# One step order for all eight batches in a fused four-stage kernel, with five subtractions moved from GpSimd to VectorE

## The reference

```python
x = x + L0(x)   # x @ W_base.T + b_base + 2 * sum_e w[b,e] * (x @ As[e].T) @ Bs[e].T
x = x + L1(x)   # x @ (sum_g y[b,g] * weight[g] * mask).T + bias
x = x + L2(x)   # two of eight experts by softmax and top-2, weighted, and one shared expert:
                #   (gelu(x @ gate) * (x @ up)) @ down,  128 -> 512 -> 128
x = x + L3(x)   # one expert by argmax: (silu(x @ W_up.T + b_up) * (x @ W_gate.T + b_gate)) @ W_down.T + b_down
```

## Time and profile before

| | us |
|---|---|
| median of three runs | 82.08 |
| profiled execution, own time | 81.98 |
| its span | 80.3 |
| TensorE busy | 75.9 |
| VectorE busy | 53.9 |
| GpSimd busy | 50.3 |
| ScalarE busy | 49.2 |

### The profile page before, as it was taken

One profiled execution on the slowest core, in us unless ns is written; L12 is line 12 of the kernel. 1 busy time (PEld: TensorE's weight loads), 2 busy tenths in 40 slices (PEclk: granted clock), 3 DMA queues, 4 the chain that ended last, 5 costly groups with the idle time before them and its releaser, 6 DMA issues.

```text
span 80.3 us, 1590 instructions
## 1 busy us (share of the span) xinstructions
PE 75.9 (95%) x480; PEld 68.0 (85%) x480; DVE 53.9 (67%) x118; ACT 49.2 (61%) x99; POOL 50.3 (63%) x48
## 2 busy tenths in 40 slices
PE   6999999999999999999994999999999999997990
PEld 6979998888888998988882989989989989996990
DVE  1489679969565638177796939499399498436371
ACT  6420796879855896737999069456496550539160
POOL 3021366298999999999999999985639910000000
DMA  1998288999999995599988998989999679882102
GB/s 17 320 380 343 45 309 328 392 426 429 425 392 411 383 395 203 126 377 347 382 226 231 361 354 295 245 316 301 382 340 270 201 179 232 289 198 63 52 21 65
DMA packets 9367, 22.17 MB, mean 276 GB/s; under 512 B 1040, under 2 KB 5776, under 8 KB 9360
## 3 DMA queue, kind: packets, MB, share of 16 engines
q1 hardware_dynamic: 9072, 21.30, 77.9%
q10 hardware_dynamic: 288, 0.79, 2.5%
HBM read 17.88 MB, written 0.52 MB: 229 GB/s over the span
## 4 chain that ended last, share of the span: by engine, by line
PE 80%; DMA 8%; SPq 5%; DVE 2%; issue 1%; ACT 1%
PE bank L964 16%; DMA x_t<-p 8%; PE bank L950 5%; PE bank L947 5%; PE bank L948 5%; PE bank L979 5%; SPq L259 5%; PE bank L900 5%; PE bank L908 5%; PE bank L916 5%; PE bank L937 4%; PE bank L994 4%; PE bank L831 4%; PE bank L839 3%; PE bank L869 2%; PE bank L923 2%
## 5 line engine op out<-in xcount | busy, mean ns | idle before, releaser
L362 POOL TENSOR_TENSOR pair_low<-pair_w,wide_h 128x512 fp32r<-128x512 f32 x18 | 22.7, 1291 | 3.2 <-ACT wide_h L457 3.2
L419 ACT ACTIVATE gelu<-bank 128x512 f32<-128x512 f32 x24 | 14.1, 594 | 10.2 <-PE bank L950 7.1
L694 DVE SCALAR_TENSOR_TENSOR hid<-gelu,wsel,bank 128x512 f32<-128x512 f32 x16 | 11.8, 735 | 6.2 <-PE bank L950 2.0
L947 PE MATMUL bank<-wide_h,x_h 128*128 128x512 f32 x28 | 11.5, 409 | 0.0
L367 POOL TENSOR_TENSOR hid_l<-hid,hid_h 128x512 fp32r<-128x512 f32 x8 | 10.2, 1289 | 1.8 <-ACT hid_h L470 1.8
L948 PE MATMUL bank<-wide_h,x_l 128*128 128x512 f32 x28 | 10.9, 390 | 0.0
L708 DVE STREAM_TRANSPOSE p<-hid 128x512 f32<-128x512 f32 x14 | 10.0, 712 | 1.1 <-DMA x_t<-p 0.7
L457 ACT ACTIVATE wide_h<-pair_w 128x512 fp32r<-128x512 f32 x18 | 10.4, 622 | 0.4 <-DMA pair_w<-in_skill 0.2
L429 ACT ACTIVATE half<-bank,half_bias 128x128 f32<-128x128 f32 x12 | 3.7, 364 | 8.7 <-PE bank L979 4.4
L692 DVE TENSOR_TENSOR hid<-gelu,bank 128x512 f32<-128x512 f32 x8 | 5.5, 685 | 3.6 <-POOL hid_l L367 2.7
L964 PE MATMUL bank<-x_t,pair_w 128*128 128x128 f32 x40 | 5.5, 280 | 1.6 <-DMA x_t<-p 1.6
(11 more groups left out here) (120 smaller groups left out, 160.1 us busy)
## 6 DMA issues: line engine op xcount, KB each, us to landing
pair_w<-in_skill SPq DMA_DIRECT2D x11, 768.0 KB, 6.9
w<-in_layer SPq DMA_DIRECT2D x6, 384.0 KB, 8.9
x_t<-p SPq DMA_DIRECT2D x16, 128.0 KB, 3.3
b_mix<-p SPq DMA_DIRECT2D x12, 128.0 KB, 4.3
shared_sb<-in_skill SPq DMA_DIRECT2D x1, 768.0 KB, 11.8
home_x<-in_skill SPq DMA_DIRECT2D x1, 768.0 KB, 12.6
home_h<-in_skill SPq DMA_DIRECT2D x1, 768.0 KB, 4.4
home_l<-in_skill SPq DMA_DIRECT2D x1, 768.0 KB, 6.6
```

Of the source, the lines that this page charges most:

```text
L362: pool.tensor_tensor(low_of(b, k)[:, m, :], w[:, m, :], wide_h[:, ring_at(b, k) % RING, m, :].bitcast(fp32), ALU.subtract).then_inc(wide_l ...
L419: act.activation(gelu[:, n, :], ps[:, :], ACT.Gelu_apprx_tanh).then_inc(gelu_ready, 1)
L694: dve.scalar_tensor_tensor(hid[:, n, :], gelu[:, n, :], wsel[:, bass.DynSlice(weight, 1)], u_ps[n][:, :], ALU.mult, ALU.mult).then_inc(hid ...
L947: pe.matmul(ps[:, :], x2_h[:, S * b:S * (b + 1)], wide_h[:, n % RING, m, :], start=True, stop=False)
```

## The change

Batch 0 joins `TURNED`: its experts are done wide, transposed and swapped as the others' are. With that the ring's places, GpSimd's and ScalarE's lists and the loads begin with batch 0. All batches now have one order of steps. Of the eight low parts of the shared hidden values, three stay on GpSimd and five go to VectorE (`hidden_rest`), in the places shown. The last batch's swap goes to a buffer of its own, two tiles of a weight home that batch 2 used, so it waits for nothing but its transposes. `layer3(6)` and `down3(5)` change places with the last batch's `down`.

```diff
-TURNED = range(1, B)
+TURNED = range(B)
+POOL_LOW = 3
...
+        hid_last = pair_w[:, 4, 0:2, :].rearrange("c m (a k s) -> c (m a) k s", k=TOP_K, s=S)
...
         def up3_ps(b, c):
+            if b == B - 2:
+                return (bank[4], bank[7])[c]
             return (bank[3], bank[2])[c] if is_last(b) else bank[7]
...
+        def hid_t_of(b):
+            return hid_last if is_last(b) else hid_t[b % 2]
...
                     sp.wait_ge(turned_ready, TOP_K * (b - TURNED[0] + 1))
-                    if b - 2 in TURNED:
+                    if is_last(b):
+                        sp.wait_ge(down_done, down_at(2, 0))
+                    elif b - 2 in TURNED:
                         sp.wait_ge(down_done, down_at(b - 2, 1))
...
-                for b, k in ((1, 0), (0, 1), (1, 1)):
-                    pick(b, k)
-                    load(b, k)
-                for b, k in ((2, 0), (2, 1), (3, 0)):
+                for b, k in ((0, 1), (1, 0), (1, 1), (2, 0), (2, 1), (3, 0)):
                     pick(b, k)
                     load(b, k)
...
+                swap(0)
                 sp.wait_ge(down_done, NSH)
                 load(4, 1)
+                swap(1)
                 load(5, 0)
                 load(5, 1)
-                swap(1)
-                sp.wait_ge(down_done, down_at(0, 0))
-                load(6, 0)
                 swap(2)
                 sp.wait_ge(down_done, down_at(0, 1))
+                load(6, 0)
                 load(6, 1)
...
-                for k in range(3):
-                    hidden_low_part(k)
-                wide_low_part(1, 0, 0)
-                hidden_low_part(3)
-                hidden_low_part(4)
-                wide_low_part(1, 0, 1)
-                hidden_low_part(5)
-                hidden_low_part(6)
-                wide_low_part(1, 1, 0)
-                hidden_low_part(7)
-                wide_low_part(1, 1, 1)
+                wide_low_part(0, 0, 0)
+                hidden_low_part(0)
+                hidden_low_part(1)
+                wide_low_part(0, 0, 1)
+                hidden_low_part(2)
+                wide_low_part(0, 1, 0)
+                wide_low_part(0, 1, 1)
...
+                rounds = {1: (0, 0, 1), 3: (0, 1, 0), 4: (0, 1, 1), 5: (1, 0, 0), 6: (1, 0, 1), 7: (1, 1, 0)}
+                round_part(0, 0, 0)
                 gelu_step(0, 0, shg_ps[0])
                 for k in range(1, NSH):
                     gelu_step(k, k % 2, shg_ps[k % 3])
                     round_hidden(k - 1)
-                    if k in (3, 4):
-                        round_part(1, 0, k - 3)
-                    if k == NSH - 1:
-                        round_part(1, 1, 0)
+                    if k in rounds:
+                        round_part(*rounds[k])
+                expert_gelu(0, 0)
                 round_hidden(NSH - 1)
-                expert_gelu(0, 0)
                 round_part(1, 1, 1)
                 expert_gelu(0, 1)
...
-                    if 2 <= k < NSH + 2:
-                        dve.wait_ge(hid_low, k - 1)
-                    elif NSH + 2 <= k < NSH + 4:
-                        dve.wait_ge(down_done, down_at(0, n))
+                    if 2 <= k < POOL_LOW + 2:
+                        dve.wait_ge(hid_low_pool, k - 1)
+                    elif POOL_LOW + 2 <= k < NSH + 2:
+                        dve.wait_ge(hid_low_dve, k - 1 - POOL_LOW)
...
+                def hidden_rest(k):
+                    dve.wait_ge(hid_high, k + 1)
+                    dve.tensor_tensor(hid_l[:, k % 3, :], hid[:, k % 2, :], hid_h[:, k % 3, :].bitcast(fp32),
+                                      ALU.subtract).then_inc(hid_low_dve, 1)
...
                 hidden(4, 0)
+                hidden_rest(3)
                 share_scale()
                 bias_halves()
                 hidden(5, 1)
+                hidden_rest(4)
                 norm_shares()
                 hidden(6, 0)
+                hidden_rest(5)
                 weight_part()
-                hidden(7, 1)
                 expert_weights()
                 settled()
-                expert_hidden(0, 0)
+                hidden(7, 1)
+                hidden_rest(6)
+                hidden(NSH, 0, 0)
+                hidden_rest(7)
+                turn(0, 0)
                 expert_hidden(0, 1)
                 add_shared(0)
                 add_shared(1)
                 expert_hidden(1, 0)
...
                 residual(B - 1)
                 gated_silu3(B - 2, 0)
+                result(B - 3, 1)
                 gated_silu3(B - 1, 1)
...
-                    if c == 0 and at_least(b, 1) and not is_last(b):
+                    if c == (1 if b == B - 2 and n == 0 else 0) and b >= 1 and not is_last(b):
                         pe.wait_ge((hid3_ready if b <= IN_BANK else half3_ready, gate3_ready)[n], HC * b)
+                    if is_last(b) and n == 1 and c == 1:
+                        pe.wait_ge(silu3_ready, 1)
...
-                gate_up(0, 0)
-                gate_up(0, 1)
+                gate_up_wide(0, 0)
+                gate_up_wide(0, 1)
                 shared_down(NSH - 3)
                 shared_down(NSH - 2)
                 shared_down(NSH - 1)
                 gate_up_wide(1, 0)
+                gate_up_wide(1, 1)
+                gate_up_wide(2, 0)
+                gate_up_wide(2, 1)
                 down(0, 0)
                 down(0, 1)
-                gate_up_wide(1, 1)
-                layer3(0)
-                gate_up_wide(2, 0)
-                gate_up_wide(2, 1)
                 gate_up_wide(3, 0)
                 gate_up_wide(3, 1)
                 down(1, 0)
-                down3(0, 0)
                 down(1, 1)
+                layer3(0)
                 gate_up_wide(4, 0)
                 gate_up_wide(4, 1)
+                down3(0, 0)
...
                 down3(B - 4, 0)
-                product3(B - 2, 0, 0, 0)
+                layer3(B - 2)
                 down(B - 1, 0)
+                down(B - 1, 1)
                 down3(B - 3, 1)
-                down(B - 1, 1)
-                pe.wait_ge(silu3_ready, 1)
-                product3(B - 2, 0, 0, 1)
-                both_chunks3(B - 2, 0, 1)
                 both_chunks3(B - 1, 1, 0)
                 both_chunks3(B - 1, 1, 1)
                 down3(B - 2, 0)
```

More of the change, by code:

```diff
@@ L156, in build @@
         sh_high, sh_low = sem("sh_high"), sem("sh_low")
-        x2_high, x2_low, hid_high, hid_low = sem("x2_high"), sem("x2_low"), sem("hid_high"), sem("hid_low")
+        x2_high, x2_low, hid_high = sem("x2_high"), sem("x2_low"), sem("hid_high")
+        hid_low_pool, hid_low_dve = sem("hid_low_pool"), sem("hid_low_dve")
         pair_in = [sem(f"pair_in{n}") for n in range(len(homes))]
@@ L255, in swap @@
                     sp.wait_ge(turned_ready, TOP_K * (b - TURNED[0] + 1))
-                    if b - 2 in TURNED:
+                    if is_last(b):
+                        sp.wait_ge(down_done, down_at(2, 0))
+                    elif b - 2 in TURNED:
                         sp.wait_ge(down_done, down_at(b - 2, 1))
                     for a in range(T):
-                        sp.dma_start(hid_t[q][:, a, :, :], turned[q][QUAD * a:QUAD * (a + 1), :, :, :]).then_inc(swapped[q], 16)
+                        sp.dma_start(hid_t_of(b)[:, a, :, :], turned[q][QUAD * a:QUAD * (a + 1), :, :, :]).then_inc(swapped[q], 16)
                 def load_w3(b, e, used=None):
@@ L367, in hidden_low_part @@
                     pool.tensor_tensor(hid_l[:, k % 3, :], hid[:, k % 2, :], hid_h[:, k % 3, :].bitcast(fp32),
-                                       ALU.subtract).then_inc(hid_low, 1)
-                for k in range(3):
-                    hidden_low_part(k)
-                wide_low_part(1, 0, 0)
-                hidden_low_part(3)
-                hidden_low_part(4)
-                wide_low_part(1, 0, 1)
-                hidden_low_part(5)
-                hidden_low_part(6)
-                wide_low_part(1, 1, 0)
-                hidden_low_part(7)
-                wide_low_part(1, 1, 1)
+                                       ALU.subtract).then_inc(hid_low_pool, 1)
+                wide_low_part(0, 0, 0)
[5 more added lines that the diff above has]
+                wide_low_part(0, 1, 1)
                 for b in TURNED[1:]:
@@ L486, in _ @@
                 expert_gelu(1, 0)
+                expert_gelu(1, 1)
                 round_pair(3, 0)
-                expert_gelu(1, 1)
+                expert_gelu(2, 0)
                 round_pair(3, 1)
-                expert_gelu(2, 0)
-                halve3(0)
-                tanh_step(0)
                 expert_gelu(2, 1)
@@ L497, in _ @@
                 expert_gelu(3, 1)
+                halve3(0)
+                tanh_step(0)
+                expert_gelu(4, 0)
                 round_pair(5, 0)
-                expert_gelu(4, 0)
+                expert_gelu(4, 1)
                 round_pair(5, 1)
-                expert_gelu(4, 1)
-                round_pair(6, 0)
```

(16 more changed lines are left out.)

## The result

The changed kernel takes 87.08 us in the median of four runs (86.7 to 89.54); the kernel before now stands at 82.59. The ratio is 1.064, with a 95% interval of 1.051 to 1.076. The forecast of 83.6 had the direction and missed the size: the time is above the range's end of 84.8, and the class that was held likeliest (within 2%, 0.51) lost to slower (0.35).

What follows compares the result with a forecast made beforehand. TensorE, busy 95% of the span, was taken as the bound. A step-by-step walk gave 81.98 − 1.8 (won on TensorE) + 2.9 (VectorE's subtractions waiting for GpSimd) + 0.5 (tail) = 83.6; 8-in-10 range 80.6 to 84.8.

Steps and rivals of the forecast that it cites:

- rest of step 3: VectorE's low-part subtraction in shared step 3: issued at 22.45, it waits for GpSimd until 23.0 and ends at 23.55.
- rest of step 4: VectorE's low-part subtraction in shared step 4: done at 26.6, while TensorE wants it at 25.8, a stall of 0.8.
- the exclusion and its price: VectorE's two-SBUF-input subtractions wait for GpSimd's running instruction and hold up its next; the five cost 2.9 us.
- Rival A: VectorE's five long subtractions take 0.69 each without waiting for GpSimd; time 80.9, chance 0.22.
- Rival B: VectorE waits for GpSimd, but GpSimd is not held up and runs on at 1.25; time 82.5, chance 0.16.
- Rival C: In shared step 3 GpSimd goes ahead of VectorE's `wnorm`, so step 4 ends 1.0 to 1.1 later; 84.7, chance 0.12.
- rest of step 6: VectorE's low-part subtraction in shared step 6: it waits for GpSimd's wide low part until 29.97 and ends at 30.5.
- no long wait for swaps: Sign expected in TensorE's changed profile: idle times near 27, 29 and 36, but none long for swapped quadrants.
- from batch 4 on TensorE has its old pattern: After batch 4's wide products start at 47.1, TensorE runs as before, with GpSimd staying ahead.
- the walk without port waits: The same step-by-step timing without VectorE waiting for GpSimd: batch 4's wide products start at 44.2 instead of 47.1.
- the tail's term: At the kernel's end, the last result waits for store 5 to land: 0.3 to 1.4 more, taken as 0.5.
- The dead home: Last swap, issued right after its transpose into an unused weight home: the 0.7 wait before `down(7, 0)` goes.

Runs made afterwards that it cites:

- experiment 2: Changed kernel with VectorE's five subtractions replaced by one-input instructions of the same length, low part left out; ratio to the kernel before 1.023.
- experiment 1: Changed kernel with swap 2 issued ahead of batch 5's two loads, nothing else changed; ratio to the kernel before 1.036, times 84.22 and 84.97.
- experiment 3: Changed kernel with one-input instructions for the five subtractions and swap 2 ahead of batch 5's loads; profiled span 81.7, one run took 81.95 us.
- experiment 9: Kernel before with only the change's end: last swap into the unused weight home, layer3(6) ahead of down(7), down3(5) and result(5) behind it; ratio 1.011.
- experiment 4: Kernel before with only the five hidden low-part subtractions moved to VectorE, batch 0 as before; ratio 1.005.

## Why the prediction was wrong

Its walk, step by step, against the changed trace:

| TensorE or VectorE | forecast | measured |
|---|---|---|
| rest of step 3 ends | 23.55 | 23.80 |
| `half_bias` ends | 24.8 | 24.98 |
| rest of step 4 ends | 26.6 | 26.75 |
| `gate_up_wide(0, 0)` | 27.5 | 27.63 |
| `gate_up_wide(0, 1)` | 29.65 | 30.11 |
| `gate_up_wide(2, 0)` | 36.65 | 37.05 |
| `down(0, 0)` | 39.65 | 40.08 |
| batch 4 | 47.1 | 47.32 |
| `down(7, 0)` (72.05 + 2.9) | 75.0 | 78.97 |
| last result after the end of `down(7, 1)` | 3.1 | 2.8 |

**Right: the exclusion and its price.** "Each ends 0.55 after the end of the GpSimd instruction in which it was issued, and holds GpSimd's next one up by 0.5": measured 0.55 and 0.46. The sum priced it at 2.9 between two walks; experiment 2 takes out 2.5. Rival A (no port waits) fell by the mean of 1.18. Rival B (GpSimd not held up) fell by the 1.76. Rival C (a lost race) did not happen: `wnorm` came first, 26.68 against 26.76, when ScalarE had rounded GpSimd's next input. One premise was wrong: GpSimd was not "never idle" but stood 0.63, 0.73 and 1.21 us between 26 and 31.3 waiting for ScalarE. So the rest of step 6 met an idle GpSimd and took 0.69, where the walk had it wait until 30.5, and that of step 7 took 1.71. `hid(7)` came later than forecast instead. That the walk held to 0.5 all the same is in part luck: such errors offset each other.

**Wrong: "no long wait for swaps" and "from batch 4 on TensorE has its old pattern".** This is the step that failed. The walk followed swaps 0 and 1 to their landing and left swap 2 out. It asked of the moved loads only whether anything holds them up, not what they hold up. Swap 2 goes behind both loads of batch 5 in the new order, while in the kernel before these were issued some five microseconds ahead of swap 1. The term stood at nothing, without a reason. A bound could have been had: at the 392 to 429 GB/s of the fullest slices on the page of before, 1.57 MB take some 3.8 us (an estimate). TensorE would have started `down(2)` at 50.6 and started at 52.6: 2.0. Experiment 1 shows the cause: with swap 2 ahead of the loads the wait is gone and the times, 84.22 and 84.97, lie at the range's end.

**Missing: the clock.** The 1.7 us at half level were in no case of the forecast. With both, the account of the profiled execution closes: 83.6 + 0.2 (batch 4 late) + 2.0 + 1.7 − 0.3 (a shorter tail) = 87.2, against 87.16. For the two runs at full clock it closes in the span: 83.6 less the 1.7 outside it is 81.9, and 81.9 + 0.2 + 2.0 − 0.3 = 83.8, against 84.1. That their times are as long all the same lies outside the traced span and is not explained.

**Too high: what the rest would bring.** The start that the walk without port waits gave, 44.2 for batch 4, was optimistic by 0.7 to 0.9, and rival A's time of 80.9 by 1.0 (experiment 3). That sum also adds 0.7 where the tail's term is 0.5, and no row gives the other 0.2. Experiments 2 and 3 still wait 0.8 for `hid(7)`, where 0.35 was taken. The dead home was priced right in itself (72.05 was to be reached without a wait; experiment 9 has none), but its gain went to store 5. The forecast's 0.5 for that store was not seen in the changed kernel, where the last result was released by TensorE 0.2 later than before; it was 0.45 in experiment 9.

**Not settled.** Why the low clock follows the wait in some executions and not in others (experiment 2 idled 2.17 without it) no run tells. Nor was it tried to put the hidden values' low part where one input comes from PSUM, which by the 684 ns of `hid<-gelu,bank` should be free of the exclusion; the kernel names all eight banks for other tiles around that stretch.

## What to carry to other kernels

Before work moves from GpSimd to VectorE, look at where its inputs lie: a VectorE instruction with two inputs in SBUF waits for the end of GpSimd's and then holds its next one up, so VectorE's idle time beside a busy GpSimd is not free time. Whether it costs the kernel anything depends on who waits behind it, as experiment 4 shows. Follow every transfer of a new order to its landing, with the bytes queued ahead of it; a swap of 512 KB behind 1.5 MB of weights that are not yet urgent is a wait in the making. And a wait of TensorE can cost more than its length: here, in one trace, the clock fell after it, for 1.7 more.

## What the runs showed of the hardware

- VectorE's two-input subtraction of 512 elements: 0.69 beside an idle GpSimd, 1.07 to 1.74 beside a busy one, ending 0.55 after GpSimd's instruction in the pairs read above. A `TENSOR_SCALAR` of 16 elements waited in the same way (1.03). The Trainium skill ("SBUF — State Buffer", "Who interferes with whom") has an instruction with two inputs in SBUF contend with GpSimd's reads, and says that `tensor_scalar` can when it enters a two-port mode. The trace agrees on the first; whether `half_bias` ran in such a mode no run here shows.
- GpSimd's instruction behind such a one takes 1.76 in place of 1.30. The Trainium skill ("SBUF — State Buffer", "SBUF: two separate sides") has the loser fully blocked; the trace agrees with 0.46, against the 0.55 that VectorE's instruction still ran.
- SyncE's own issue of a swap's four transfers takes 2.5 to 3.1 elsewhere in the changed kernel's trace. It took 3.79 behind the two loads of batch 5 (3.49 in experiment 2), but only 2.49 for swap 3 behind four loads in experiment 1, so the bytes queued ahead do not settle it alone.
- A 128 KB transfer of a swap landed 2.8 us after its issue with no load issued between it and the swap before (experiment 1), 6.0 to 6.7 behind two loads of 768 KB just issued (the changed kernel, experiment 2), and 6.9 to 9.2 behind four (experiments 1 and 3).
